# Second attention in rounds of four units in place of two

## The chip, the cores and the metric

One core of one Trainium2 chip runs the whole program. The metric is the device time of one execution in microseconds (us). The core has TensorE (PE: matmuls, and PEld: the loads of their stationary operand), VectorE (DVE), ScalarE (ACT), GpSimd (POOL) and the DMA queues that SyncE (SP) and ScalarE issue. Engines run apart from each other and are tied by counters ("semaphores"): an instruction adds to a counter when it is done, and another engine waits until the counter has reached a number. Each engine works through its own list in order.

## The reference

The program is two blocks on an input of 2 x 256 channels x 32 x 32. The first is a deformable attention with a learned bias network and an MLP; the change does not touch it. The second is a plain attention:

```
xf  = x as (batch, 1024 tokens, 256)
qkv = xf @ W_qkv + b_qkv                 # 8 heads of 32
att = softmax over j of (q_i . k_j) / sqrt(32)
out = (att @ v) @ W_out + b_out + xf
```

There are 2 batches x 8 heads = 16 heads, and each has a 1024 x 1024 matrix of scores.

## The kernel before

The second attention cuts each head's scores into 8 units of 128 rows, so there are 128 units (`SLOTS`); unit s belongs to head s // 8. Every unit is computed twice:

- `along(x)` (L1203): two matmuls of 512 columns give scores with 128 queries on the partitions. VectorE takes the largest of each row (`maxes(x)`, L863) to find the softmax's shift. This runs `AHEAD_MAX` = 14 units ahead.
- `across(s)` (L1233): two matmuls of 512 columns give scores the other way round, with 128 keys on the partitions and the shift already subtracted by two more rows of the operand. ScalarE takes the exponential of the 1024 columns into one of six slots `PT` (L658 and L659 in halves for even units, L661 in one for odd ones).
- `weigh(s)` (L1244): the values of 128 keys times `PT`. The four quarters of the columns go to four column tiles of 32 in the array. The trace counts 8 matmuls of 256 columns for a unit.
- GpSimd adds the two `PT` slots of a pair of units (L484) into one of two buffers `PSUMS`, and `sums(j)` (L1254) sums that over the keys with a matrix of ones: 8 matmuls in the same column tiles, for each pair of units.

Once per head, eight units apart: `turn(n)` (L1214) transposes the maxima, ScalarE (L645) and VectorE (L868) split them in two parts, and SP's queue moves these into the rows of the queries (L366). VectorE takes four reciprocals of the sums, one behind each of four consecutive `maxes` (`invert`, L877), and one product behind the next (`divide`, L885). Then SP moves the head's result to where the projection reads it (L374), and the slots of queries and keys are loaded for a head to come (SP's L360, ScalarE's L616, which sits behind the exponential of the head's last unit).

PSUM has eight banks. Banks 6 and 7 hold the results of `weigh` and `sums`. Banks 0 to 5 are three pairs, a ring through which the across and along units go in the order in which TensorE issues them: across, along, across, along, and so on. So an item needs the pair of the item three before it to be read. The waits in the code say this:

```python
# across(s), x = s + 14
elif s > 1 and x - 1 <= SLOTS:
    pe.wait_ge(mx_ready, x - 1)      # maxes of along(x - 2) are done
# along(x)
pe.wait_ge((half_ready, pr_ready)[hf], ((x - AHEAD_MAX + 1) // 2, x - AHEAD_MAX)[hf])
# exponential of unit s
act.wait_ge(pv_done, s - PRING + 1)           # weigh(s - 6)
act.wait_ge(added, (s - PRING) // 2 + 1)      # addition of that pair
# addition j
pool.wait_ge(sums_done, j - 1)                # sums(j - 2)
```

TensorE's order is written out by a loop over rounds (L1273 to L1286). A round before is: across, along, across, along, then `weigh` of the two units of the round before it, then `sums` of the pair before that.

Of the kernel before, what the change touches and what calls it, by code (L numbers as in the profile page):

```python
# [50 lines left out]
SLOTS = G * NK  # L51
# [11 lines left out]
def build(nc, d, out):  # L63
# [5 lines left out]
    with ctx:  # L69
# [99 lines left out]
        def bank(i, n=1):  # L169
            return ps[:, 512 * i:512 * (i + n)]  # L170
# [67 lines left out]
        def turning(x):  # L238

            return TURN <= x < TURN + SLOTS and (x - TURN) % NK == 0  # L240

        def turned(x):

            return min(max((x - TURN) // NK + 1, 0), G)
# [668 lines left out]
        def _(pe):  # L913
# [269 lines left out]
            def along(x):  # L1183

                n, it = x // NK, x % NK
                if it == 0:
                    pe.wait_ge(st_in[n % HEADS3], 96 * (n // HEADS3 + 1))
                if 2 <= x < AHEAD_MAX and not turning(x - 1):
                    pe.wait_ge(mx_ready, x if turning(x) else x - 1)
                elif 2 <= x < AHEAD_MAX:  # L1190
                    pe.wait_ge(m_lo, 1)
                elif x < 2:
                    pass
                elif turning(x):
                    pe.wait_ge(mx_ready, x)
                elif x == AHEAD_MAX:
                    pe.wait_ge(mx_ready, x - 1)
                elif x % 2 == 0:
                    pe.wait_ge(pr_ready, x - AHEAD_MAX)
                for hf in range(2):  # L1200
                    if x > AHEAD_MAX and x % 2 == 1:
                        pe.wait_ge((half_ready, pr_ready)[hf], ((x - AHEAD_MAX + 1) // 2, x - AHEAD_MAX)[hf])
                    last = pe.matmul(bank(2 * along_pair(x) + hf), QS[n % HEADS3][0:ROWS, P * it:P * (it + 1)],  # L1203
                                     KS[n % HEADS3][0:ROWS, HALF * hf:HALF * (hf + 1)], start=True, stop=True)
                last.then_inc(sc_ready, 1)

            def turn(n):

                pe.wait_ge(mx_ready, NK * (n + 1))
                if n < G - 1:  # L1210
                    pe.wait_ge(mx_ready, TURN + NK * n - 1)
                else:
                    pe.wait_ge(pr_ready, TURN + NK * n - AHEAD_MAX - 2)
                pe.transpose(bank(2 * turn_pair(n))[0:NK, 0:P], amax[n % HEADS3][:, :], ident[:, :]).then_inc(tr_ready, 1)  # L1214

            def across(s):

                n, kt = s // NK, s % NK
                if kt == 0:
                    pe.wait_ge(m_in, 32 * (n + 1))  # L1220
                x = s + AHEAD_MAX
                if turning(x):
                    pe.wait_ge(pr_ready, s)
                elif turning(x - 1):
                    pe.wait_ge(m_lo, turned(x))
                elif s == 0:
                    pe.wait_ge(mx_ready, AHEAD_MAX)
                elif s > 1 and x - 1 <= SLOTS:
                    pe.wait_ge(mx_ready, x - 1)
                elif s > 1:  # L1230
                    pe.wait_ge(pr_ready, s - 2)
                for hf in range(2):
                    last = pe.matmul(bank(2 * across_pair(s) + hf), KS[n % HEADS3][0:ROWS + 2, P * kt:P * (kt + 1)],  # L1233
                                     QS[n % HEADS3][0:ROWS + 2, HALF * hf:HALF * (hf + 1)], start=True, stop=True)
                last.then_inc(st_ready, 1)

            def weigh(s):

                n, kt = s // NK, s % NK
                if kt == 0 and n >= 2:  # L1240
                    pe.wait_ge(o_done, n - 1)
                pe.wait_ge(pr_ready, s + 1)
                for c in range(4):
                    last = pe.matmul(bank(6 + n % 2)[D * c:D * (c + 1), 0:QUARTER], V[:, n, kt, :],  # L1244
                                     PT[s % PRING][:, QUARTER * c:QUARTER * (c + 1)],
                                     start=(kt == 0), stop=(kt == NK - 1), skip_group_check=True)
                last.then_inc(pv_done, 1)

            def sums(j):

                n = j // (NK // 2)
                pe.wait_ge(added, j + 1)
                for c in range(4):
                    last = pe.matmul(bank(6 + n % 2)[D * c:D * (c + 1), QUARTER:2 * QUARTER], ones[:, :],  # L1254
                                     PSUMS[j % 2][:, QUARTER * c:QUARTER * (c + 1)],
                                     start=False, stop=(j % (NK // 2) == NK // 2 - 1), skip_group_check=True)
                last.then_inc(sums_done, 1)
# [12 lines left out]
                along(x)  # L1270
            pe.wait_ge(vv_saved, 2 * NK)
            pe.wait_ge(ones_ready, 1 + HEADS3)
            for r in range(SLOTS // 2 + 2):  # L1273
                for s in (2 * r, 2 * r + 1):
                    x = s + AHEAD_MAX
                    if turning(x):
                        turn(turned(x) - 1)
                    if s < SLOTS:
                        across(s)
                    if x < SLOTS:  # L1280
                        along(x)
                if 0 < r <= SLOTS // 2:
                    weigh(2 * r - 2)
                    weigh(2 * r - 1)
                if r >= 2:
                    sums(r - 2)  # L1286

            pe.wait_ge(mx_ready, SLOTS)
            pe.wait_ge(pr_ready, SLOTS)
# [70 lines left out]
```

## Time and profile before

| | us |
|---|---|
| median of 3 runs | 1280.26 (1278.66 to 1280.81) |
| profiled execution, its own time | 1279.23 |
| its span, from the first to the last instruction | 1277.3 |
| second attention's rounds within the span | about 1023.7 to 1260.1 |
| final projection | about 1260.1 to 1277.3 |

The profile comes from one execution. Times of instructions count from the start of its span. TensorE is busy for 96% of the span, VectorE for 63%, ScalarE for 65% and GpSimd for 54%. The ends of matmuls are modelled, since they are pipelined.

### The profile page before, as it was taken

To read this page: it belongs to the slowest core of one execution; us is meant where nothing else is said; L and a number is where in the kernel's file an instruction comes from. 1 tells how busy PE (TensorE), PEld (TensorE's weight loads), DVE (VectorE), ACT (ScalarE), POOL (GpSimd) and SP (SyncE) were. 2 spreads that over 40 slices of the span, in tenths; PEclk is the share of its full clock that TensorE was granted. 3 is DMA by queue.
4 is the path that set the end of the run, shared out by engine and by line. 5 is a ranking of instruction groups with operands and counts; after the bars stand their busy time and mean duration, and the time that the engine had idled before them with its cause. 6 is when DMAs were issued, how large, how long until landed. Compare 5 with 4: busy or idle time off the path is not lost.

```text
span 1277.3 us, 25474 instructions
## 1 busy us (share of the span) xinstructions
PE 1224.8 (96%) x10548; PEld 539.0 (42%) x10548; DVE 800.3 (63%) x1026; ACT 834.7 (65%) x1024; POOL 695.0 (54%) x391
## 2 busy tenths in 40 slices
PE   6499999999999999999999999898999899999998
PEld 4333333333333333333333333656886555555554
DVE  6766666666666666666666665554332677777773
ACT  4678777777777777887778877447442355555552
POOL 3366666666666666666666665250000056666664
PEclk9589999999999999999999999998999999999999
DMA  2340110111011011011001100000004413222212
GB/s 76 97 145 2 34 34 1 35 34 31 4 34 34 1 35 35 1 35 34 25 11 34 34 1 2 1 1 1 1 1 165 172 38 71 61 61 61 60 36 78
DMA packets 22507, 51.67 MB, mean 40 GB/s; under 512 B 5622, under 2 KB 10870, under 8 KB 22264
## 3 DMA queue, kind: packets, MB, share of 16 engines
q1 hardware_dynamic: 20084, 43.74, 12.2%
q10 hardware_dynamic: 2308, 6.30, 2.0%
q8 instruction: 84, 1.38, 0.4%
q14 instruction: 31, 0.25, 0.1%
HBM read 36.64 MB, written 11.15 MB: 37 GB/s over the span
## 4 chain that ended last, share of the span: by engine, by line
PE 90%; DVE 4%; ACT 2%; DMA 1%; POOL 1%; issue 1%; SPq 0%; POOLq 0%; DVEq 0%; ACTq 0%
PE ps L999 34%; PE ps L1008 18%; PE ps L1203 6%; PE ps L1233 5%; PE ps L990 5%; PE ps L1244 5%; PE ps L1136 4%; PE ps L1121 3%; PE ps L1165 2%; PE ps L1254 2%; PE ps L1298 1%; PE ps L1179 1%; DVE big L711 1%; PE ps L1021 1%; PE ps L1024 1%
## 5 line engine op out<-in xcount | busy, mean ns | idle before, releaser
L999 PE MATMUL ps<-big,w 64*64 64x512 f32 x2736 | 324.0, 590 | 0.0
L558 ACT ACTIVATE big<-ps 128x1024 f32<-128x1024 f32 x172 | 176.2, 1024 | 87.7 <-PE ps L999 87.7
L770 DVE TENSOR_SCALAR big<-big 128x1024 f32<-128x1024 f32 x171 | 118.7, 694 | 169.2 <-POOL big L447 169.2
L447 POOL TENSOR_TENSOR big<-qpad 128x1024 f32<-128x1024 f32 x86 | 164.3, 1911 | 96.6 <-DVE big L770 28.7
L764 DVE TENSOR_TENSOR big<-qpad,ps 128x1024 f32<-128x1024 f32 x171 | 207.4, 1213 | 1.2 <-PE ps L969 1.2
L447 POOL TENSOR_TENSOR big<-qpad,V 128x1024 f32<-128x1024 f32 x85 | 162.4, 1910 | 80.2 <-DVE ring L770 28.8
L558 ACT ACTIVATE big<-ps,vec 128x1024 f32<-128x1024 f32 x172 | 190.6, 1108 | 0.1
L863 DVE TENSOR_REDUCE amax<-ps 128x1 f32<-128x1024 f32 x128 | 154.0, 1210 | 43.2 <-PE ps L1203 42.4
L999 PEld LDWEIGHTS ps<-big,w 64*64 64x64 f32 x2736 | 98.0, 133 | 151.8 <-issue 85.5
L1008 PE MATMUL ps<-big,w3s 128*32 128x512 f32 x1376 | 160.4, 595 | 0.0
L999 PE MATMUL ps<-ring,w 64*64 64x512 f32 x1360 | 160.4, 588 | 0.0
L484 POOL TENSOR_TENSOR big<-big 128x1024 f32<-128x1024 f32 x32 | 76.4, 2387 | 98.2 <-ACT big L661 58.2
L558 ACT ACTIVATE ring<-ps 128x1024 f32<-128x1024 f32 x84 | 86.0, 1024 | 39.9 <-PE ps L999 39.9
L770 DVE TENSOR_SCALAR ring<-ring 128x1024 f32<-128x1024 f32 x85 | 59.0, 694 | 84.4 <-POOL ring L447 84.4
L447 POOL TENSOR_TENSOR ring<-qpad,V 128x1024 f32<-128x1024 f32 x43 | 82.1, 1910 | 40.6 <-DVE big L770 28.8
L764 DVE TENSOR_TENSOR ring<-qpad,ps 128x1024 f32<-128x1024 f32 x85 | 103.1, 1213 | 0.0
L447 POOL TENSOR_TENSOR ring<-qpad 128x1024 f32<-128x1024 f32 x42 | 80.2, 1910 | 39.7 <-DVE big L770 27.8
L990 PE MATMUL ps<-S,wl 57*64 57x512 bf16 x1024 | 100.9, 384 | 0.0
L484 POOL TENSOR_TENSOR BT<-big 128x1024 f32<-128x1024 f32 x32 | 76.4, 2388 | 38.5 <-PE ps L1254 37.3
L658 ACT ACTIVATE big<-ps 128x512 f32<-128x512 f32 x64 | 38.3, 598 | 87.6 <-PE ps L1233 87.6
L558 ACT ACTIVATE ring<-ps,vec 128x1024 f32<-128x1024 f32 x84 | 93.0, 1107 | 0.0
L1008 PEld LDWEIGHTS ps<-big,w3s 128*32 128x32 f32 x1376 | 40.3, 109 | 111.6 <-issue 86.4
(179 smaller groups left out, 1680.8 us busy)
## 6 DMA issues: line engine op xcount, KB each, us to landing
raw<-s_f SPq DMA_DIRECT2D x32, 512.0 KB, 5.9
h1l<-k_d SPq DMA_DIRECT2D x33, 128.0 KB, 3.6
h1h<-q_d ACTq DMA_DIRECT2D x33, 128.0 KB, 4.2
X<-in_x SPq DMA_DIRECT2D x2, 1024.0 KB, 6.1
q_d<-XN SPq DMA_DIRECT2D x4, 512.0 KB, 3.1
k_d<-XN SPq DMA_DIRECT2D x4, 512.0 KB, 3.4
q_d<-big SPq DMA_DIRECT2D x4, 512.0 KB, 3.6
k_d<-big SPq DMA_DIRECT2D x4, 512.0 KB, 3.8
```

Source lines behind the costliest of these rows:

```text
L447: pool.tensor_tensor(h1[m % HRING].rearrange("p (y a b) -> p y a b", y=2, b=W), u.unsqueeze(2).to_broadcast(shape), a[:, :, HALF // W * hf ...
L484: pool.tensor_tensor(PSUMS[j % 2], PT[2 * j % PRING], PT[(2 * j + 1) % PRING], ALU.add).then_inc(added, 1)
L558: act.activation(h2[m % H2RING], z2[m % ZRING], ACT.Relu, bias=v("cb2") if m % 2 else 0.0).then_inc(h2_ready, 1)
L764: dve.tensor_tensor(h1[m % HRING].rearrange("p (y a b) -> p y a b", y=2, b=W), u.unsqueeze(2).to_broadcast(shape), b[:, :, HALF // W * hf: ...
L770: dve.tensor_scalar(h1[m % HRING], h1[m % HRING], 0.0, None, ALU.max).then_inc(h1_ready, 1)
L863: dve.tensor_reduce(amax[n % HEADS3][:, it:it + 1], bank(2 * along_pair(x), 2), AX.X, ALU.max, negate=True).then_inc(mx_ready, 1)
L990: pe.matmul(z2[m % ZRING][CH * y:CH * (y + 1), HALF * x:HALF * (x + 1)], wl1[CH * x:CH * x + KROWS, 2 * w + y, :], S[CH * x:CH * x + KROWS ...
L999: last = pe.matmul(z2[m % ZRING][CH * y:CH * (y + 1), HALF * x:HALF * (x + 1)], w2[CH * x:CH * (x + 1), :], h1[m % HRING][CH * x:CH * (x + ...
L1008: last = pe.matmul(zb[32 * k:32 * (k + 1), :], w3s[:, a:a + 32], h2[(m + k // 2) % H2RING][:, HALF * (k % 2):HALF * (k % 2 + 1)], start=(m ...
L1203: last = pe.matmul(bank(2 * along_pair(x) + hf), QS[n % HEADS3][0:ROWS, P * it:P * (it + 1)], KS[n % HEADS3][0:ROWS, HALF * hf:HALF * (hf ...
L1233: last = pe.matmul(bank(2 * across_pair(s) + hf), KS[n % HEADS3][0:ROWS + 2, P * kt:P * (kt + 1)], QS[n % HEADS3][0:ROWS + 2, HALF * hf:HA ...
L1244: last = pe.matmul(bank(6 + n % 2)[D * c:D * (c + 1), 0:QUARTER], V[:, n, kt, :], PT[s % PRING][:, QUARTER * c:QUARTER * (c + 1)], start=( ...
```

## The change

The loop takes four units for a round in place of two: across and along four times in turn, then four `weigh`, then two `sums`. Round r issues the across of units 4r to 4r + 3 with their alongs, `weigh` of units 4r - 2 to 4r + 1, and `sums` of pairs 2r - 2 and 2r - 1. The same instructions run, in another order on TensorE; no wait, buffer, size or other engine's list is changed.

```diff
-            for r in range(SLOTS // 2 + 2):
-                for s in (2 * r, 2 * r + 1):
+            for r in range(SLOTS // 4 + 1):
+                for s in range(4 * r, 4 * r + 4):
                     x = s + AHEAD_MAX
                     if turning(x):
                         turn(turned(x) - 1)
...
-                if 0 < r <= SLOTS // 2:
-                    weigh(2 * r - 2)
-                    weigh(2 * r - 1)
-                if r >= 2:
-                    sums(r - 2)
+                for s in range(4 * r - 2, 4 * r + 2):
+                    if 0 <= s < SLOTS:
+                        weigh(s)
+                for j in (2 * r - 2, 2 * r - 1):
+                    if j >= 0:
+                        sums(j)
```

## Rows read from the trace of the kernel before

**Rows 1.** Busy time by stretch: stretch, length, engines' busy time, granted clock, DMA share, GB/s.

```profile
1031.00:1234.60 203.60, 203.57 (x1746) 112.36 (x1742) 158.28 (x186) 112.00 (x176) 128.68 (x54) 1.00 0.25 60
```

**Rows 2.** Chain that ended last: start, us, what; last along of a pair, first and last.

```profile
1032.65 0.74 PE ps L1203 x2
...
1236.31 0.74 PE ps L1203 x2
```

**Rows 3.** The same chain through one pair of units, from the first across.

```profile
1102.69 0.66 PE ps L1233 x2
1103.34 0.47 PE ps L1203 x2
1103.82 0.47 PE ps L1233 x2
1104.28 0.73 PE ps L1203 x2
1105.02 1.00 PE ps L1244 x16
1106.02 0.43 PE ps L1254 x8
```

**Rows 4.** Timeline of that pair: start, us, engine, line, work, [idle before <-what ended it].

```profile
1103.38 0.60 ACT L658 ACTIVATE big<-ps 128x512 f32<-128x512 f32 x1 [1.77 <-PE ps L1233]
1103.85 2.43 DVE L863 TENSOR_REDUCE amax<-ps 128x1 f32<-128x1024 f32 x2 [1.08 <-PE ps L1203]
1103.88 0.59 ACT L659 ACTIVATE big<-ps 128x512 f32<-128x512 f32 x1
...
1104.52 0.19 PEld L1203 LDWEIGHTS ps<-h1l,h1h 96*128 96x128 f32 x1 [0.30 <-ACT big L659]
...
1106.63 2.39 POOL L484 TENSOR_TENSOR BT<-big 128x1024 f32<-128x1024 f32 x1 [1.38 <-PE ps L1254]
```

**Rows 5.** Timeline of the opening, where eight items follow each other: its last items.

```profile
1027.54 2.36 DVE L863 TENSOR_REDUCE amax<-ps 128x1 f32<-128x1024 f32 x2 [0.48 <-PE ps L1203]
...
1028.82 0.30 PEld L1233 LDWEIGHTS ps<-h1h,h1l 98*128 98x128 f32 x2 [0.69 <-DVE amax L863]
...
1029.40 0.63 PE L1203 MATMUL ps<-qk 96*128 96x512 f32 x2
```

**Rows 6.** Timeline of VectorE around a division, and around the first reciprocal of four.

```profile
1100.09 1.22 DVE L863 TENSOR_REDUCE amax<-ps 128x1 f32<-128x1024 f32 x1 [0.56 <-PE ps L1203]
1101.23 0.41 DVE L885 TENSOR_TENSOR big<-ps,big 128x256 f32<-128x256 f32 x1
1101.56 1.21 DVE L863 TENSOR_REDUCE amax<-ps 128x1 f32<-128x1024 f32 x1
...
1107.63 1.23 DVE L863 TENSOR_REDUCE amax<-ps 128x1 f32<-128x1024 f32 x1 [0.36 <-PE ps L1203]
1108.77 0.55 DVE L877 RECIPROCAL big<-ps 128x64 f32<-128x64 f32 x1
1109.23 1.16 DVE L863 TENSOR_REDUCE amax<-ps 128x1 f32<-128x1024 f32 x1
```

**Rows 7.** Timeline: queries' load issued by ScalarE, and the one along that waited longest for it.

```profile
1217.46 0.36 ACTq L616 DMA_DIRECT2D h1h<-q_d  x1
...
1224.06 0.30 PEld L1203 LDWEIGHTS ps<-h1l,h1h 96*128 96x128 f32 x2 [0.47 <-DMA h1h<-q_d]
```

**Rows 8.** Timeline of the end, from the across of unit 112 to the last sums.

```profile
1234.64 0.30 PEld L1233 LDWEIGHTS ps<-qk 98*128 98x128 f32 x2 [0.41 <-issue]
...
1246.57 0.76 PEld L1233 LDWEIGHTS ps<-h1h,h1l 98*128 98x128 f32 x4 [0.41 <-issue]
...
1247.70 0.59 PEld L1244 LDWEIGHTS ps<-big 128*32 128x32 f32 x16 [0.37 <-issue]
...
1257.10 2.35 POOL L484 TENSOR_TENSOR BT<-big 128x1024 f32<-128x1024 f32 x1 [0.17 <-ACT big L661]
...
1259.50 0.16 PEld L1254 LDWEIGHTS ps<-BT,ones 128*32 128x32 f32 x8 [1.81 <-POOL BT L484]
```

## The prediction

> **What bounds the kernel now.** I first read the busy time by stretch, to see whether the stage of the change has an engine that sets its pace. From 1031 to 1234.6 us TensorE is busy for all of 203.60 us at a granted clock of 1.00 (2.4 GHz), VectorE for 158.28 and GpSimd for 128.68 [rows 1]. So TensorE sets the order, but a busy TensorE can hold waits, since ends of matmuls are modelled. The chain that ended last shows the period: the last along of a pair starts at 1032.65 and, 54 pairs later, at 1236.31 [rows 2]. That is 3.771 us for a pair and 7.54 for four units, in every part of the stage.
>
> Within one pair the chain gives the parts [rows 3]: across 0.66, along 0.47, across 0.47, along 0.73, two weighs (16 matmuls) 1.00, sums (8 matmuls) 0.43; together 3.76. Three things are to be seen. A full-size item that follows another takes 0.47; the first one behind the small tiles takes 0.19 more. The second along takes 0.73 because its second half waits until ScalarE has read the first across: VectorE and ScalarE read the ring, and here that costs 0.26 [rows 3, 4]. And a matmul of the small tiles takes 0.43 / 8 = 0.0537 where it follows its like, so 16 would take 0.86 and the switch to them costs 0.14.
>
> From here t is counted from the end of the last sums (1102.69). The first along ends at 1.13 (1103.82), VectorE starts on it at 1.16 and needs 2.43 for the two maxima [rows 3, 4]. It ends the second at 3.59, when TensorE has long been at weigh. So now the slower reader works off its queue behind weigh and sums, and the next round finds the ring empty.
>
> **The change part by part.** *Switches.* One of two visits to the small tiles is dropped for each four units: 0.19 + 0.14 = 0.33 us saved [rows 3], the only gain that I see. The Trainium skill, "TensorEngine Tiling (Array Packing)", Key Properties, says that changing the tiling mode drains TensorE; by that rule alone 27 rounds would be the shorter for it, 1271 us, an estimate from these two rows, and the faster rival below is its case.
>
> *Items five to eight of a round.* With the ring of three pairs, the third across needs the first maximum, and the fourth across needs the second. The reader's queue, which weigh and sums cover now, comes onto TensorE's path. The kernel before has one place where eight items follow each other, its opening [rows 5]: the load for the fourth across waits 0.69 for VectorE and goes at 1028.82, 0.06 after the second maximum can have ended (1027.54 + 1.22), and the along behind it ends at 1030.03, 1.21 later. The same in the new rounds: second maximum 3.59, plus 0.06, plus 1.21: the fourth along ends at t = 4.86. By ScalarE it would be the same: the third across goes at 2.38 + 0.05 and ends 0.74 later; two halves of the exponential take 1.09 [rows 4], and the last half of the along 0.50 more, so 4.84. The opening had a lower clock at its start, but its last along shows 0.63 for two matmuls [rows 5].
>
> That rows show the reading of PSUM as the bound is also what the Trainium skill says against packing such work closer, same page, PSUM Bottleneck: tiling speeds up TensorE and not the evacuation of PSUM. As an estimate by that rule, four maxima of 1.21 make 4.84 at the least; the trace's waits give 4.86, and the sum stands on these.
>
> *Weigh and sums.* Four weighs and two sums are 48 small matmuls: 1.00 + 0.86 + 2 x 0.43 = 2.72. I take 0.0537 for each of the 24 added ones from the sums, which follow 16 others in the same tiles. Bounds: 0.037, the pace of the weight loads (0.59 / 16, [rows 8]), or 0.0625, the 1.00 / 16 of a weigh with its switch. The round's time is then 4.86 + 2.72 = 7.58.
>
> *VectorE's other work.* Now it is covered. In the new rounds what stands between the first and the second maximum comes on the path, as the fourth across waits for the second. Each head has four reciprocals, behind the maxima of alongs 26 + 8n to 29 + 8n; these go with units 12 + 8n to 15 + 8n, which are all four of an odd round. The product follows the first maximum of the next, even round. From the start of the first maximum to the end of the second it is 2.76 with the reciprocal (1107.63 to 1110.39) and 2.68 with the product (1100.09 to 1102.77) [rows 6], against 2.43 plain [rows 4]. So an odd round takes 7.58 + 0.33 = 7.91, an even one 7.58 + 0.25 = 7.83. Bounds: nothing, if the readers hide it, or the whole 0.55 and 0.41. The transposed maxima come once in an odd round, at its start, where the ring is empty; they are priced at nothing, since the opening pair of such a round has the same pace now [rows 2].
>
> *The stage.* Round 0 has the order of before, with its eight items and the same two weighs. Rounds 1 to 27 are full: two plain ones, 13 with reciprocals, 12 with a product: 2 x 7.58 + 13 x 7.91 + 12 x 7.83 = 211.95. Before, 27 x 7.54 = 203.65. **Loss 8.3 us.**
>
> *Queued behind.* GpSimd's additions need sums of two pairs earlier. Both now come at the end of a round. The first addition starts 0.18 after its sums (1106.63 against 1106.45, [rows 3, 4]), so at t = -0.25, and ends at 2.14; the second ends at 4.53. The third exponential starts at 3.20 and needs the first; the second sums, at 7.1, needs the second. Both are hidden, by 1 us and 2.5. The queries of a head to come are issued behind the last exponential of an odd round (t = 4.8) and needed by the third along of the even one, 5.9 later. The slowest load of before landed 6.60 after its issue [rows 7], so that along can be 0.7 late; the fourth across behind it waits until 3.90 for VectorE anyway, which covers it. Price: nothing.
>
> *The end.* From unit 114 on there are no alongs; before, a pair takes 2.56 (1.13 from 1246.57 to the weigh at 1247.70, and 1.00 + 0.43), and GpSimd's 2.39 is nearly the pace. From the across of unit 112 to the last sums it is 1259.50 - 1234.64 = 24.86 [rows 8]. In rounds of four: round 28 still has two alongs and a product; its fourth across goes at 3.97, the weighs 0.67 later (1.13 for two across, less 0.46), and it lasts 4.64 + 2.72 = 7.36. In rounds 29 to 31 the fourth across waits for the first exponential, 1.92 after the start; the weighs begin at 2.59, and a round lasts 5.3. So the weighs of round 31 begin at 7.36 + 2 x 5.3 + 2.59 = 20.55. Only behind four weighs comes sums 60, for which GpSimd's addition 62 waits: it starts at 23.1, and 62 and 63 take 2 x 2.39 (now they start as soon as ScalarE is done, with 0.17 of idle time). The last sums come at 27.9. **Loss 3.1 us**, bounds 0 and 5. The projection behind it is unchanged.
>
> The sum: 8.3 + 3.1 = 11.4 us. The profiled execution's own time is 1279.23 (span 1277.3), which gives 1290.6; it lies 1.0 below the median of 1280.26, so on the median 1291.7.
>
> **The rivals.** *VectorE's extras are hidden*: the products and reciprocals don't delay the second maximum. Then 13 x 0.33 + 12 x 0.25 = 7.3 less: 1284.4. For it: they cost nothing now. Against: they stand in VectorE's list between the two maxima, and the delay shows there [rows 6].
>
> *The small matmuls run at the pace of their weight loads* when many follow each other: 24 x (0.0537 - 0.037) = 0.4 less a round, 10.8 in all: 1280.9, no change that can be told. Against: the eight sums took 0.43 in the chain.
>
> *Faster: the ring's waits don't grow.* If readers keep pace and the eight items cost what two lots of four cost now, less one switch [rows 3], the fourth along ends at 2.33 + 2.33 - 0.19 = 4.47, and a round gains 0.33 (0.19 before it, 0.14 behind it): 27 x 0.33 = 8.9, less 3.1 lost at the end, 1274.5. It decides from a fourth along that ends before 7.54 - 2.72 = 4.82. Against: the opening's 0.69 wait, and two maxima that alone end at 3.59. The rule of the Trainium skill that a change of tiling mode drains TensorE ("TensorEngine Tiling (Array Packing)", Key Properties) speaks for this case.
>
> *Worse*: each pair of weighs takes 1.00 also when it follows another (27 x 0.14 = 3.8) and the extras weigh in whole, 13 x 0.22 + 12 x 0.16 = 4.8 more: 1300.3.
>
> **How the numbers follow.** My forecast 0.70 (1287 to 1297), extras hidden 0.09, weight-load pace 0.06, faster 0.07, worse 0.08. The range 1283.5 to 1297.5 takes in the forecast, the case of hidden extras and some of the worse one; outside it stay the pace of weight loads and the faster case, 0.13, with a few hundredths above. Slower by over 0.2% (2.6 us, about what a measurement of this kernel can tell from no change): 0.70 + 0.09 + 0.08 + a little of the weight-load case, 0.88. Within 0.2%: 0.05. Faster: 0.07.
>
> **What the profile after would show.** Right: TensorE's weight loads for the third and fourth across wait for VectorE's maxima in nearly every round; a round takes some 7.9 with reciprocals, 7.8 with a product; 32 weigh matmuls in a row take 1.86 in the chain; GpSimd idles before each pair of additions and runs two back to back; the granted clock stays at 1.00. Wrong: if the fourth across goes with no wait, the ring is not the bound; if odd and even rounds are alike at 7.6, the extras were hidden; if sums begin 1.4 after the first weigh, small matmuls are limited by weight loads; if the last sums come 25 us after unit 112, the end costs nothing.

## The result and the profile after

The changed kernel takes 1294.78 us (median of 4 runs, 1293.50 to 1295.84) against 1279.81 for the kernel before: a ratio of 1.0117, 95% interval 1.0099 to 1.0134. It is slower, by 15.0 us where 11.4 were forecast. The profiled execution has a span of 1292.8 us, 15.5 more than before.

The chain that ended last, through one even round and the start of the odd one behind it, in the kernel after (start, us, what), is to be laid beside [rows 3]:

```profile
1100.82 0.66 PE ps L1233 x2
1101.48 0.48 PE ps L1203 x2
...
1101.99 0.04 DVE amax L863
1102.02 1.11 issue
1103.13 0.10 DVE big L885
1103.23 0.23 issue
1103.46 1.23 DVE amax L863
1104.69 0.04 issue
1104.73 0.73 PE ps L1233 x2
1105.46 0.46 PE ps L1203 x2
1105.92 1.86 PE ps L1244 x32
1107.79 0.86 PE ps L1254 x16
1108.65 0.20 PE ps L1214
...
1110.97 0.55 DVE big L877
1111.52 1.09 DVE amax L863
1112.61 0.04 issue
1112.65 0.74 PE ps L1233 x2
```

Before, this chain never left TensorE within a pair. Now it goes from the first along (ends 1101.96) to VectorE: first maximum, product, second maximum, and back to the fourth across at 1104.73. In the odd round a reciprocal stands in the product's place. The four weighs take 1.86 and the two sums 0.86. The even round lasts 1108.65 - 1100.82 = 7.83.

TensorE's weight loads in the kernel after (start, us, engine, line, work, [idle before <-what ended it]):

```profile
1103.27 0.30 PEld L1233 LDWEIGHTS ps<-qk 98*128 98x128 f32 x2 [0.42 <-DVE amax L863]
...
1104.73 0.30 PEld L1233 LDWEIGHTS ps<-qk 98*128 98x128 f32 x2 [0.70 <-DVE amax L863]
...
1108.58 0.08 PEld L1214 LDWEIGHTS ps<-ident,amax 128*8 128x8 f32 x1 [0.41 <-issue]
...
1112.65 0.30 PEld L1233 LDWEIGHTS ps<-qk 98*128 98x128 f32 x2 [0.77 <-DVE amax L863]
...
1124.35 0.08 PEld L1214 LDWEIGHTS ps<-ident,amax 128*8 128x8 f32 x1 [0.41 <-issue]
```

The third and the fourth across wait for VectorE. From one transposed maximum (L1214) to the next, two rounds, it is 1124.35 - 1108.58 = 15.77, where four pairs took 15.08 before.

Busy time by stretch in the kernel after (columns as in [rows 1]):

```profile
1031.00:1243.00 212.00, 201.52 (x1742) 113.11 (x1741) 155.98 (x186) 114.50 (x175) 124.73 (x54) 1.00 0.25 58
...
1247.30:1251.00 3.70, 3.70 (x41) 1.84 (x44) 0.00 (x0) 1.02 (x1) 0.00 (x0) 0.54 0.10 26
...
1268.00:1272.10 4.10, 1.15 (x20) 0.19 (x12) 0.00 (x0) 0.00 (x0) 4.06 (x2) 0.89 0.02 5
1272.10:1278.00 5.90, 5.89 (x14) 2.39 (x15) 2.97 (x6) 0.00 (x0) 0.00 (x0) 0.50 0.04 11
```

The third figure from the end is the granted clock. In the stage it is 1.00 (2.4 GHz), as before. At the end it is near 0.5 (1.2 GHz) twice: in the weighs of round 28 and at the start of the projection, behind a stretch in which TensorE was busy for 1.15 of 4.10 us, waiting for GpSimd. The timeline of the same end:

```profile
1242.61 0.30 PEld L1233 LDWEIGHTS ps<-qk 98*128 98x128 f32 x2 [0.41 <-issue]
...
1246.60 0.30 PEld L1233 LDWEIGHTS ps<-qk 98*128 98x128 f32 x2 [1.16 <-DVE amax L863]
...
1247.27 3.61 PE L1244 MATMUL ps<-big 128*32 128x256 f32 x32
...
1254.26 1.93 PE L1244 MATMUL ps<-big 128*32 128x256 f32 x32
...
1269.80 0.16 PEld L1254 LDWEIGHTS ps<-big,ones 128*32 128x32 f32 x8 [1.77 <-POOL big L484]
...
1272.11 0.20 PEld L1254 LDWEIGHTS ps<-BT,ones 128*32 128x32 f32 x8 [2.15 <-POOL BT L484]
```

Thirty-two weigh matmuls take 3.61 in round 28 and 1.93 in round 29: 1.68 us for the lower clock. From the across of unit 112 to the last sums it is 1272.11 - 1242.61 = 29.50, against 24.86 before [rows 8]; without the 1.68 it would be 27.82, 2.96 more than before. From the last sums to the end of the span it is 1292.8 - 1272.11 = 20.7, against 1277.3 - 1259.5 = 17.8.

So the 15.5 us of span are: the rounds from 1 to 27, 1242.61 - 1030.32 = 212.29 against 1234.64 - 1030.97 = 203.67 between the same points (the start of round 1 and of unit 112), +8.6; the late sums, +3.0; the clock in round 28, +1.7; the projection, +2.9; and what comes before the rounds, -0.65.

### The profile page after: what moved, and what is told of

Same layout as the page of the kernel before. It is cut to its first block, busy times and chain, and to the rows that moved or that the text cites. A ratio compares the mean times of both kernels' runs of the same rounds, so it can differ in the third digit from the quotient of the medians.

```text
span 1292.8 us, 25474 instructions
## 1 busy us (share of the span) xinstructions
PE 1225.9 (95%) x10548; PEld 539.9 (42%) x10548; DVE 798.3 (62%) x1026; ACT 837.5 (65%) x1024; POOL 693.9 (54%) x391
## 4 chain that ended last, share of the span: by engine, by line
PE 84%; DVE 7%; issue 3%; ACT 2%; POOL 1%; DMA 1%; SPq 0%; POOLq 0%; DVEq 0%; ACTq 0%
PE ps L999 34%; PE ps L1008 18%; PE ps L990 5%; PE ps L1244 5%; PE ps L1233 4%; PE ps L1136 4%; DVE amax L863 3%; PE ps L1121 3%; PE ps L1203 3%; PE ps L1165 2%; PE ps L1254 2%; PE ps L1299 1%; PE ps L1179 1%; DVE big L711 1%; PE ps L1021 1%
## 5 line engine op out<-in xcount | busy, mean ns | idle before, releaser
L447 POOL TENSOR_TENSOR big<-qpad 128x1024 f32<-128x1024 f32 x86 | 164.4, 1912 | 96.6 <-DVE ring L770 27.9
L764 DVE TENSOR_TENSOR big<-qpad,ps 128x1024 f32<-128x1024 f32 x171 | 207.6, 1214 | 1.2 <-PE ps L969 1.2
L764 DVE TENSOR_TENSOR ring<-qpad,ps 128x1024 f32<-128x1024 f32 x85 | 103.2, 1214 | 0.0
L1008 PE MATMUL ps<-ring,w3s 128*32 128x512 f32 x672 | 80.3, 595 | 0.0
```

The costliest lines, as they stand in the source:

```text
L447: pool.tensor_tensor(h1[m % HRING].rearrange("p (y a b) -> p y a b", y=2, b=W), u.unsqueeze(2).to_broadcast(shape), a[:, :, HALF // W * hf ...
L764: dve.tensor_tensor(h1[m % HRING].rearrange("p (y a b) -> p y a b", y=2, b=W), u.unsqueeze(2).to_broadcast(shape), b[:, :, HALF // W * hf: ...
L1008: last = pe.matmul(zb[32 * k:32 * (k + 1), :], w3s[:, a:a + 32], h2[(m + k // 2) % H2RING][:, HALF * (k % 2):HALF * (k % 2 + 1)], start=(m ...
```

## The experiments

**VectorE's extras moved.** Theory: the 25 rounds with reciprocals or a product are long since these stand ahead of the second maximum. Rival: another reason, such as ScalarE's reading or the order on TensorE.

```diff
-                if 0 <= n < G and c < 4:
+                if 0 <= n < G and 1 <= c < 4:
+                    if c == 1:
+                        invert(n, 0)
                     invert(n, c)
-                elif 0 <= n < G and c == 4:
+                elif 0 <= n < G and c == 5:
                     divide(n)
```

> The changed order, but VectorE's four reciprocals of a head and its product stand behind the second, third and fourth maximum of a round and none between the first and the second. Theory (VectorE's queue between first and second maximum holds the fourth across): the 25 rounds that have one of them lose 0.25 or 0.33 us each, every round of four takes about 7.58, and the time falls by 7.3 us from 1294.8 to about 1287.5. Rival (the rounds are long for another reason, such as ScalarE's reading or the order on TensorE): the time stays within 1 us of 1294.8.

Measured: 1282.80 us (10 runs), a ratio of 1.0031 (1.0020 to 1.0042) to the kernel before. The chain of this kernel:

```profile
1113.38 0.67 PE ps L1235 x2
...
1114.55 1.24 DVE amax L863
...
1115.82 0.73 PE ps L1235 x2
1116.56 0.47 PE ps L1205 x2
...
1117.04 0.73 PE ps L1235 x2
1117.77 0.46 PE ps L1205 x2
1118.23 1.86 PE ps L1246 x32
1120.10 0.86 PE ps L1256 x16
1120.96 0.20 PE ps L1216
```

The round is 1120.96 - 1113.38 = 7.58, and no product or reciprocal stands in the chain. The fourth along of this round also waits 0.17 us for ScalarE (second half, at 1117.73): without the extras the two readers end nearly level, as the prediction's 4.86 and 4.84 say. Between the transposed maxima of heads 2 and 14 it takes 182.2 us in place of 189.2: the 7 us that the theory says.

The time fell by 12, though, to below the 1287.5 expected; of the other 5, 4.6 are what the clock costs the kernel after. In 8 of the 10 runs the mean clock (the granted clock, averaged over the span) is 0.980 or 0.981, with 1281.5 to 1283.4 us; the two others have 0.976 and 0.977, with 1286.7 and 1286.3. The profiled run has a granted clock of 1.00 to the end. Its end has the same waits of 1.77 and 2.15 us ahead of the last sums, and these are its stretches there:

```profile
1258.20:1262.30 4.10, 1.15 (x20) 0.18 (x12) 0.00 (x0) 0.00 (x0) 4.05 (x2) 1.00 0.02 5
1262.30:1268.20 5.90, 5.89 (x21) 2.61 (x22) 3.62 (x7) 0.00 (x0) 0.00 (x0) 1.00 0.06 17
```

TensorE is busy for 1.15 of 4.10 us, as in the kernel after, and here the clock does not fall.

**The end in rounds of two**, and **both edits together**. Theory: the end's loss is the late sums and the clock that follows from TensorE's waits there. Rival: the rounds of four bring the lower clock.

```diff
-            for r in range(SLOTS // 4 + 1):
+            for r in range(28):
...
+            for r in range(56, SLOTS // 2 + 2):
+                for s in (2 * r, 2 * r + 1):
...
+                if r <= SLOTS // 2:
+                    weigh(2 * r - 2)
+                    weigh(2 * r - 1)
+                sums(r - 2)
```

> The changed order up to unit 111, and from unit 112 on the rounds of two of before. Theory (the end loses by sums that come late for GpSimd, and the lower granted clock at weigh of round 28 and in the projection follows from TensorE's waits there): the end takes 24.9 us again in place of 29.5, the projection 17.8 in place of 20.7, and the time falls by 7.5 us to about 1287.3. Rival (the lower clock comes from the rounds of four in the stage and stays): only the 3 us of the late sums come back, 1291.8.

> Both: VectorE's extras moved behind the second maximum, and the end in rounds of two. Theory: the two losses add up, 7.3 + 7.5, so that the time is about 1280, that of before, with rounds of 7.58 against 7.54 before. Rival (the two prices overlap, or the rounds of four have a loss of their own beside them): 1284 or more.

Measured: 1287.75 us (ratio 1.0064, 1.0047 to 1.0080) with the end alone, 1280.33 us (1.0010, 1.0001 to 1.0020) with both. The end is that of before to the hundredth from the last transposed maxima to the last sums: 1268.45 - 1249.92 = 18.53, and 1259.50 - 1240.97 = 18.53 before. With both, the time is 14.5 below the kernel after, about the 7.0 of the extras and the 7.6 of the end, clock included. What is left, 1.1 us, fits rounds of 7.58 in place of 7.54 (27 x 0.04). The falls of the two kernels by themselves, 12.0 and 7.0, make more, since each has lost the lower clock. As it went with the extras moved too, where the end was left as it is, the end in rounds of two does not show what brings it.

**Half of the readers.** Theory: VectorE's reading of PSUM bounds the round of four, ScalarE's is next. Rival: ScalarE's. Three kernels read half of the columns: VectorE alone, ScalarE alone, both; and a fourth does both in the rounds of two. The results of the attention are those of halves.

```diff
-                dve.tensor_reduce(amax[n % HEADS3][:, it:it + 1], bank(2 * along_pair(x), 2), AX.X, ALU.max, negate=True).then_inc(mx_ready, 1)
+                dve.tensor_reduce(amax[n % HEADS3][:, it:it + 1], bank(2 * along_pair(x), 2)[:, 0:HALF], AX.X, ALU.max, negate=True).then_inc(mx_ready, 1)
```

ScalarE's edit for the odd units; the two halves of an even unit are halved in the same way:

```diff
...
-                    act.activation(PT[s % PRING], bank(2 * across_pair(s), 2), ACT.Exp).then_inc(pr_ready, 1)
+                    act.activation(PT[s % PRING][:, 0:HALF], bank(2 * across_pair(s), 2)[:, 0:HALF], ACT.Exp).then_inc(pr_ready, 1)
...
```

> The changed order, and VectorE takes the maxima over the first 512 of the 1024 columns only (the other half of the maxima is left out). Theory (VectorE's reading of the along units is the bound of the rounds of four, ScalarE next): no across waits for VectorE any more, the fourth along waits for the third exponential and ends at 4.5 us in place of 5.1 to 5.2, a round takes about 7.2, and the time falls by 18 us to about 1276.5. Rival (ScalarE's reading is the bound already): no change, 1294.8.

> The changed order, and ScalarE takes the exponential of half of the columns of each unit only (the other half is left out). Theory (VectorE is the bound): rounds with reciprocals or a product stay at 7.8 to 7.9, only the units at the end without maxima gain, and the time is 1292 to 1295. Rival (ScalarE's reading is the bound): the fourth along comes 0.4 us earlier in every round, 1284 or less.

> The changed order with both reductions of the reading: maxima over half of the columns and exponentials of half of the columns (the other halves are left out). Theory (all that the rounds of four lose comes from the readers of PSUM): nothing waits within the eight items, which take 0.66 + 7 x 0.47 = 3.95, a round takes 6.67, and the stage is 0.33 a round shorter than that of the same reductions in rounds of two: about 1261. Rival (the order has a price of its own on TensorE): a round stays above 7.0, and the time above 1270.

> The kernel before, rounds of two, with the same two reductions (half of the columns left out of the maxima and of the exponentials). Theory: a pair takes 0.66 + 3 x 0.47 + 1.43 = 3.50 in place of 3.77, the time is about 1265, and the rounds of four with the same reductions have the shorter stage, 6.67 against 7.00 for four units, by the switch saved, though their end is 5 to 7 us longer. Rival (the switch saves nothing): the stages are alike.

One run each: 1268.26, 1289.15, 1255.05 and 1259.74 us, beside 1277.39 in the one run of the kernel before. Two rounds (four pairs in the last kernel), from one transposed maximum to the next, take 14.43, 15.76, 13.78 (mean of twelve) and 14.01 (mean of the first eight; later ones wait for a head's queries), against 15.77 after. With half of the maxima alone no across waits for a maximum; with half of the exponentials alone they wait as long as in the kernel after:

```profile
1112.44 0.30 PEld L1233 LDWEIGHTS ps<-qk 98*128 98x128 f32 x2 [0.78 <-DVE amax L863]
```

So VectorE is the bound of these rounds. ScalarE is next, at 7.2 us a round: with half of the maxima, 52 loads of the alongs between 1027 and 1214 us wait for an exponential's second half. The time of the second kernel fell by 5.6 all the same, below the 1292 to 1295 expected: its profile has no lower clock at the end (the projection takes 17.9). The other three times are 5 to 8 us below those expected, though the first kernel's round is the expected 7.2. In that kernel 4.6 us of this is again the clock, and 3.5 is the opening, which no sum had counted: the second transposed maximum comes at 1026.82 in place of 1030.32. In the last two kernels it comes at 1023.35 and 1024.42. With both reductions the rounds of four are the faster ones, 13.78 against 14.01 for two, but not 13.34 as expected. The chain through such a round:

```profile
1107.77 0.47 PE ps L1203 x2
1108.24 0.59 PE ps L1233 x2
1108.82 0.47 PE ps L1203 x2
1109.29 0.53 PE ps L1233 x2
1109.82 0.47 PE ps L1203 x2
1110.28 1.86 PE ps L1244 x32
1112.15 0.86 PE ps L1254 x16
```

The third and fourth across still take 0.59 and 0.53 in place of 0.47: some wait is left, and once a head the load of an along waits 0.15 to 0.49 us for the queries. In these two single runs 0.12 of the 0.33 us a round comes out as gain.

**Early half of the exponential**, in the rounds of two and in the rounds of four. Theory: in rounds of two ScalarE's reading holds the second along; in rounds of four VectorE's holds the fourth across. So the same edit should gain in one and not in the other. The first lines stand in across, in the loop over its two matmuls, and act behind the first; the others stand in ScalarE's loop.

```diff
+ if hf == 0 and s % 2 == 0:
+     last.then_inc(st_half, 1)
...
- act.wait_ge(st_ready, s + 1)
+ act.wait_ge(*((st_half, s // 2 + 1) if s % 2 == 0 else (st_ready, s + 1)))
  act.activation(PT[s % PRING][:, 0:HALF], bank(2 * across_pair(s)), ACT.Exp).then_inc(half_ready, 1)
+ act.wait_ge(st_ready, s + 1)
```

> The kernel before, rounds of two, with one edit: for even units ScalarE starts the first half of the exponential when the first of the two matmuls of across is done, and not when both are; the second half still waits for both. Theory (in the rounds of two the second along waits for the first across to be read by ScalarE, 0.26 us a pair): the read ends 0.2 us earlier, a pair takes about 3.53 in place of 3.77, and the time falls by some 13 us from 1279.8 to 1267. Rival (ScalarE's reading is not what sets the pair): no change, 1279.8.

> The changed order with the early start of the exponential's first half for even units, which took 11 us off the rounds of two. Theory (in the rounds of four VectorE's maxima hold the fourth across, and ScalarE's reading ends earlier than that): rounds with reciprocals or a product stay at 7.8 to 7.9, and the time stays within 2 us of 1294.8. Rival (ScalarE's reading is the bound in either order): about 0.2 us a round, 5 us or more, is gained, 1289 or less.

Measured: 1268.59 us in rounds of two, a ratio of 0.9919 (0.9903 to 0.9935) to the kernel before: it beats both. In rounds of four it is 1292.63 us, and two rounds take 1124.37 - 1108.62 = 15.75, as without the edit. The time lies 2.2 below 1294.8, just outside the 2 us expected, and 1.2 below the 1293.78 of the kernel after that was run beside it; its profile has the lower clock in the projection and not in round 28, where 32 weighs take 1.94. The weight loads of the rounds of two, at the transposed maxima and at two waits:

```profile
1103.40 0.08 PEld L1216 LDWEIGHTS ps<-ident,amax 128*8 128x8 f32 x1 [0.41 <-issue]
...
1117.56 0.08 PEld L1216 LDWEIGHTS ps<-ident,amax 128*8 128x8 f32 x1 [0.41 <-issue]
...
1171.98 0.30 PEld L1205 LDWEIGHTS ps<-h1l,h1h 96*128 96x128 f32 x2 [1.01 <-DMA h1h<-q_d]
...
1186.77 0.30 PEld L1205 LDWEIGHTS ps<-h1l,h1h 96*128 96x128 f32 x2 [0.84 <-DMA h1h<-q_d]
```

A pair takes (1117.56 - 1103.40) / 4 = 3.54 at first, as expected; the second along takes 0.51 in the chain in place of 0.74. From 1160 us on, a head takes 14.8 to 15.0 in place of 14.17, since the queries of a head to come land late. That is the new wait; over four heads it takes 2.7 of the 13 us. Why it comes only from then on is not shown.

**The kernel after again**, and **with its waits filled**: two extra matmuls ahead of each of the last two sums, so that TensorE works where it waited. The two waits in the edit are met long before.

```diff
                 for j in (2 * r - 2, 2 * r - 1):
+                    if j >= SLOTS // 2 - 2:
+                        pe.wait_ge(mx_ready, SLOTS)
+                        pe.wait_ge(pr_ready, SLOTS)
+                        for kt in range(CT):
+                            pe.matmul(bank(0), wout[:, kt, 0:P], X[:, kt, 0:HALF], start=(kt == 0), stop=(kt == CT - 1))
```

> The changed kernel as it is, again, beside the two others of this group. Theory (three terms: the stage's rounds +8.6 us, the end's late sums +3.0, and a granted clock of 1.2 GHz for a few us at the end +4.6, which depends on where TensorE's waits fall): most runs lie at 1293 to 1296 with a mean clock of 0.976, and a run without the lower clock would lie at 1290 to 1291 with a clock of 0.980. Rival (the lower clock has nothing to do with the time): the times don't follow the mean clock.

> The changed order, with two extra matmuls of 512 columns, whose result nobody reads, ahead of each of the last two sums, where TensorE waits 1.8 and 2.2 us for GpSimd. They add work and no result. Theory (the lower clock in the projection follows from TensorE's waits ahead of the last two sums): the projection runs at 2.4 GHz, takes 17.8 us in place of 20.7, and the time falls by 2.9 us to about 1291.9 though there is more work. Rival (the lower clock has another cause): 1294.8 or more.

Measured: 1293.78 us again (ratio 1.0111, 1.0091 to 1.0131). Three of its four runs have 0.977 and 1293.2 to 1294.9 us; the fourth has 0.981 and 1289.72. With the waits filled it is 1291.61 us (ratio 1.0099, 1.0082 to 1.0116), every run at 0.979 to 0.981, and the projection runs at 2.4 GHz, as the stretches of that kernel show. The last line is its weighs of round 28, from the timeline:

```profile
1268.00:1273.00 5.00, 5.00 (x26) 1.70 (x25) 0.88 (x2) 0.00 (x0) 2.56 (x2) 1.00 0.02 3
1273.00:1289.00 16.00, 12.91 (x31) 5.39 (x29) 7.25 (x12) 0.00 (x0) 0.00 (x0) 1.00 0.38 139
...
1247.46 1.94 PE L1244 MATMUL ps<-big 128*32 128x256 f32 x32
```

The filled kernel does more work, and its median is 2.2 us lower than that of the kernel after beside it; the two intervals overlap. Its time fits the theory, but does not show it. In its profile the weighs of round 28 run at the full clock too, and they are done over 15 us before the first extra matmul, which cannot have brought that about. And the same two waits of 1.77 and 2.15 us stand in seven profiles without extra matmuls. In three the clock falls behind them (the kernel after, the same again, the early half in rounds of four). In four it stays at 1.00 (the extras moved, and the three kernels of half readers in rounds of four), with TensorE as busy, 1.14 to 1.16 of the 4.10 us ahead of the last sums. So these waits alone do not bring the clock down. What does, there and in round 28, stays open.

## Why the prediction was right

*Items five to eight of a round, and VectorE's other work.* Right in place and size: the third and fourth across wait for the maxima, an even round takes 7.83, two rounds 15.77 (15.74 forecast), and a round with the extras moved 7.58. The stage lost 8.6 us where 8.3 were forecast (27 x 7.54 is 203.58, which makes the forecast 8.4). The rival of hidden extras falls with the moved ones. The Trainium skill states that tiling speeds up TensorE and not the evacuation of PSUM ("TensorEngine Tiling (Array Packing)", PSUM Bottleneck). The trace agrees as far as it goes: TensorE's order changed, a maximum took 1.20 us (1.21 before), and two rounds fall from 15.77 to 14.43 by half of the maxima alone. That the estimate of four maxima, 4.84, lies so near 4.86 is chance: the fourth along ends when three maxima are done (1105.92 in the even round above), and the fourth maximum is taken while the weighs run.

*Weigh and sums.* 1.86 + 0.86 = 2.72, to the hundredth; 32 weight loads take 1.45 of the 1.86, so their pace is not the limit.

*Queued behind.* As forecast it costs nothing: GpSimd idles 3.2 us ahead of a pair of additions and runs two back to back (1100.57 to 1105.29), and no along in the rounds of four waits for a head's queries.

*Switches.* The gain is there, and hidden: with half of the reading, rounds of four are shorter than rounds of two by 0.12 us each. By the Trainium skill's rule that a change of tiling mode drains TensorE ("TensorEngine Tiling (Array Packing)", Key Properties) alone, the kernel would have been faster. The trace agrees that something is paid at a switch, 0.66 in place of 0.47 for the first across behind the small tiles and 1.86 for 32 weighs in place of 2 x 1.00, and shows that this did not bound the round.

*The end.* 3.0 us for late sums where 3.1 were forecast (27.9 - 24.86 is 3.04). The path is the forecast one: without the 1.68 us of the clock, the weighs of round 31 begin 20.6 us after the across of unit 112 (at 1264.86; 20.55 forecast), and addition 62 after 23.1 (at 1267.40), as forecast. Edits that end in rounds of two have the old end.

*The step that was mis-sized* is "the granted clock stays at 1.00", in what the profile after would show: it holds in the stage and not at the end. I priced the waits ahead of the last sums as time only. Behind them the clock was at 1.2 GHz in the projection (2.9 us), and it fell in round 28 too (1.7): 4.6 us that the sum has no term for, and whose cause the runs leave open. The one run of the changed kernel with a mean clock of 0.981, 1289.72, is 10.4 above the 1279.31 of the kernel before beside it, close to the 11.4 of the sum; the others lie some 4 us higher. The forecast of 1291.7 lies between. So the 11.4 us are right by their mechanism, and the 3.6 us missing to the measured 15.0 are the clock's, of whose 4.6 the 0.65 ahead of the rounds takes a part back.

## What to carry to other kernels

Before items are batched to save a switch, write down the ring that they pass through: items beyond its depth wait for its readers, and whatever stands in a reader's list ahead of the item waited for (here a product or a reciprocal, 0.6 us in two rounds) comes onto the path. And the faster way was in the first profile: 0.26 us a pair in which the last item waited for a reader that could have started one matmul earlier.

## What the runs showed of the hardware

In the kernel after, the granted clock fell to 0.50 for some 6 us behind the waits of 1.77 and 2.15 us ahead of the last sums, which made the projection 2.9 us longer, and it was 0.54 in the weighs of round 28, which took 3.61 us in place of 1.93. The fall is not certain in a given run: 7 of this kernel's 8 runs have the lower mean clock, and 2 of 10 with the extras moved, whose end has the same waits. Behind equal waits, with TensorE busy for 1.14 to 1.16 of 4.10 us, the clock stayed at 1.00 in four profiles and fell to 0.50 in three; what decides it was not found.

Small matmuls of 256 columns in column tiles took 0.0537 us each in the chain when their like stand before them, and kept that pace over 48 in a row (1.86 + 0.86, less the first switch).
